# A Perceiver layer (attention, gated mixing, top-2 mixture of experts): router chain moved up by one batch, and a new order of work behind the loop

## The reference, cut to what matters

```
x = x + xattn(layernorm(x), ctx)          # 16 heads of 8, softmax over 257 keys
u = layernorm(x)                          # per batch of 32 rows:
xf = [u[0], u[1:] @ WB.T]; xb = [u[1:] @ WBf.T, u[-1]]
gamma = sigmoid(xf @ w1.T + xb @ w2.T + b)
x = x + gamma * (xf + xb) + (1 - gamma) * u
h = layernorm(x); logits = h @ gate        # 8 experts
w, e = top_k(logits, 2); w = softmax(w)
x = x + sum_k w_k * (silu(h @ w0[e_k]) * (h @ w1[e_k])) @ wo[e_k]
```

## Time and profile before

| what | us |
|---|---|
| median of 3 runs (lowest, highest) | 249.22 (248.66, 250.11) |
| the profiled execution, its own time | 247.98 |
| its span on the core | 246.2 |
| PE busy in the span | 211.2 (86%) |
| DVE, ACT, POOL busy | 145.7, 140.3, 131.0 |
| mean granted PE clock | 0.944 |

### The profile page before, as it was taken

How to read it: one execution, slowest core, us unless ns; L and a number is a source line. 1 busy time by engine, 2 the same in 40 slices (tenths; PEclk the granted TensorE clock), 3 DMA queues, 4 the chain that set the end, 5 groups by cost and what they waited for, 6 DMA issues and landing times.

```text
span 246.2 us, 6768 instructions
## 1 busy us (share of the span) xinstructions
PE 211.2 (86%) x2071; PEld 179.7 (73%) x2071; DVE 145.7 (59%) x521; ACT 140.3 (57%) x465; POOL 131.0 (53%) x334
## 2 busy tenths in 40 slices
PE   7789998999999999999994985539809999999970
PEld 7567777878777787778773684539809899999970
DVE  2788778788797887987968473234502123222602
ACT  2478878979888788887895642022402343444310
POOL 2874576854687686776864954062441233334303
PEclk9999999999999999999998699576977999999999
DMA  7799450500504600000002154304434877777053
GB/s 200 284 374 326 162 170 3 170 3 7 169 24 150 196 23 4 13 11 3 22 5 89 50 175 109 108 23 134 103 130 141 270 222 225 215 229 232 34 171 89
DMA packets 17763, 31.19 MB, mean 127 GB/s; under 512 B 2350, under 2 KB 9649, under 8 KB 17728
## 3 DMA queue, kind: packets, MB, share of 16 engines
q1 hardware_dynamic: 16112, 28.10, 36.5%
q0 software_dynamic: 1184, 2.12, 2.5%
q10 hardware_dynamic: 432, 0.54, 0.7%
HBM read 22.07 MB, written 9.01 MB: 126 GB/s over the span
## 4 chain that ended last, share of the span: by engine, by line
PE 53%; POOL 11%; DMA 11%; DVE 9%; issue 8%; ACT 4%; SPq 1%; POOLq 1%; ACTq 0%; DVEq 0%
PE bank L1119 13%; PE bank L1129 7%; PE bank L927 6%; PE bank L917 6%; PE bank L957 5%; PE bank L884 5%; PE bank L886 4%; DMA table<-rows_tok,slot_at 4%; DMA slot_sb<-table 3%; ACT p_sb L721 2%; DVE neg_max L1248 2%; POOL table L601 2%; DMA pt_sb<-planes 2%; POOL tile_rstd L556 2%; DMA vec_sb<-vectors 2%
## 5 line engine op out<-in xcount | busy, mean ns | idle before, releaser
L721 ACT ACTIVATE p_sb<-bank,neg_max 128x257 f32<-128x257 f32 x128 | 59.0, 472 | 21.6 <-DVE neg_max L1248 21.5
L1248 DVE TENSOR_REDUCE neg_max<-bank 128x1 f32<-128x257 f32 x128 | 48.6, 424 | 11.1 <-PE bank L996 5.2
L1119 PE MATMUL bank<-slot_ft,w_now 128*128 128x128 f32 x368 | 50.9, 287 | 0.6 <-issue 0.6
L1119 PEld LDWEIGHTS bank<-slot_ft,w_now 128*128 128x128 f32 x368 | 48.0, 204 | 1.6 <-issue 1.2
L667 POOL DMA_INDIRECT planes<-y_sb,y_row x21 | 20.8, 992 | 37.3 <-ACT y_sb L814 35.9
L1510 DVE TENSOR_TENSOR hid_ft<-silu_sb,bank 128x512 f32<-128x512 f32 x23 | 15.8, 687 | 37.0 <-PE bank L1119 36.1
L730 ACT ACTIVATE pt_sb<-bank 128x512 f32<-128x512 f32 x64 | 35.1, 612 | 1.2 <-PE bank L927 1.2
L927 PE MATMUL bank<-ident,p_sb 128*128 128x128 f32 x256 | 34.1, 277 | 0.0
L814 ACT ACTIVATE y_sb<-bank,zero_rows,slot_meta 128x128 f32<-128x128 f32 x23 | 10.5, 457 | 34.5 <-PE bank L1129 34.5
L927 PEld LDWEIGHTS bank<-ident,p_sb 128*128 128x128 f32 x256 | 29.7, 144 | 0.3 <-issue 0.3
L917 PE MATMUL bank<-kv_sb,qbd_sb 32*128 32x257 f32 x256 | 24.6, 425 | 3.5 <-ACT p_sb L721 1.4
(11 more groups left out here) (179 smaller groups left out, 333.9 us busy)
## 6 DMA issues: line engine op xcount, KB each, us to landing
w_now<-w SPq DMA_DIRECT2D x23, 512.0 KB, 4.0
table<-empty_rows SPq DMA_DIRECT2D x3, 1300.0 KB, 10.0
ctx_sb<-ctx_keys SPq DMA_DIRECT2D x7, 512.0 KB, 3.9
wo_sb<-wo SPq DMA_DIRECT2D x8, 256.0 KB, 4.3
slot_sb<-table SPq DMA_DIRECT2D x23, 65.0 KB, 2.8
planes<-zero_rows SPq DMA_DIRECT2D x2, 512.0 KB, 6.7
pt_sb<-planes SPq DMA_DIRECT2D x4, 256.0 KB, 4.8
table<-empty_rows SPq DMA_DIRECT2D x1, 975.0 KB, 10.1
```

The costliest lines, as they stand in the source:

```text
L721: act.activation(p_sb[b % 2][:, g, :], s_bank[g][:, 0:SKV], ACT.Exp, bias=neg_max[b % 2][:, g:g + 1], accum_out=sum_last[:, 0, b, g:g + 1] ...
L1119: last = pe.matmul(bank[2 * m + s % 2][:, tile(c)], w01_now[s % W_BUFS][:, m, tile(c)], slot_ft[s % 2][:], start=True, stop=True)
L1248: dve.tensor_reduce(neg_max[b % 2][:, g:g + 1], s_bank[g][:, 0:SKV], AX.X, ALU.max, negate=True).then_inc(max_ready, 1)
```

## The change

It has these parts (core of the diff below):

1. The six chain constants are one less, so that each chain step comes one batch earlier; `scale_tile`, `spread_scales`, `spread` and the taking of the spread scales also come one batch earlier. On POOL `spread_scales` moves to r = 0, ahead of `residual`; `count_experts` and `edges` are at r = 0 behind both; `tile_root(0)` is at r = 3, ahead of `queries`; `store_rows` is at r = 2.
2. The router works on the transposed unnormalised tile (`x2_tok`) and a centred gate matrix (`gate_c`, one product at b = 7); the softmax weight takes the inverse deviation as a scale. `turn_rows` waits for `x2_ready`, not for `rows_normed`.
3. `plan` is split in three parts; of `plan(0)` part 0 stands at the end of b = 29 and part 1 at the end of b = 30.
4. Behind the loop: another order on every engine, `keep_meta` and `number_output` are gone (row numbers and weights are read from the loaded rows, which have 131 columns instead of 130), the last `spread` writes to bank 1, four slot tiles (`LATE_TURNS`, one each) are transposed at the end of an iteration.
5. SP: 5 weight buffers and 8 row buffers; in each stage up to three weight loads are issued ahead of the row loads, in stage 0 too.
6. The planes are interleaved by token, read back with two DMAs of 512 KB; DVE adds the first pair, POOL the second.

```diff
-W_BUFS = 3
+W_BUFS = 5
-        WO_AT, TURN_AT, MIX_AT, ROW_TURN_AT, LOGITS_AT, RANKS_AT = 7, 8, 9, 11, 12, 13
+        WO_AT, TURN_AT, MIX_AT, ROW_TURN_AT, LOGITS_AT, RANKS_AT = 6, 7, 8, 10, 11, 12
@@ SP, in each stage
-                load_weights(first)
+                for s in range(first, heavy):          # heavy = min(end, first + 3)
+                    load_weights(s)
                 for i in range(stored, last_tile + 1):
                     sp.wait_ge(rows_stored[i], 16 * TOPK)
@@ SP, end
+            pairs = planes.rearrange("(p t c) d -> p t c d", p=128, c=TOPK)
             for n in range(2):
-                for c in range(TOPK):
-                    sp.dma_start(planes_sb[c][:, half_tiles(n), :], ...)
+                sp.dma_start(pairs_sb[n], pairs[:, half_tiles(n), :, :]).then_inc(pair_in[n], 16)
@@ POOL, loop over b
                 if r == 0 and b >= BPT:
+                    spread_scales(b // BPT - 1)
                     residual(b // BPT - 1)
...
                 if at(b, WO_AT + 1) is not None:
                     tile_root(0, at(b, WO_AT + 1))
                 if at(b, LOGITS_AT + 1) is not None:
                     count_experts(at(b, LOGITS_AT + 1))
                 if at(b, TURN_AT + 1) is not None:
                     edges(at(b, TURN_AT + 1))
-                if r == 1 and b > BPT:
-                    spread_scales(b // BPT - 1)
                 if at(b, MIX_AT + 1) is not None:
                     mix_residual(at(b, MIX_AT + 1))
                     tile_root(1, at(b, MIX_AT + 1))
                 if r == 3 and b // BPT + 1 < NT:
                     queries(b // BPT + 1)
@@ POOL, behind the loop
             add_heads(B - 2)
             add_heads(B - 1)
+            tile_root(0, NT - 2)
             count_experts(NT - 3)
             mix_residual(NT - 2)
+            edges(NT - 2)
+            keep_slots(NT - 3)
+            store_rows(NT - 3, 0)
             tile_root(0, NT - 1)
+            store_rows(NT - 3, 1)
+            mix_residual(NT - 1)
+            edges(NT - 1)
             tile_root(1, NT - 2)
@@ PE
             def turn_rows(i, dst):
-                pe.wait_ge(rows_normed, i + 1)
-                pe.transpose(dst[:, C_TURN], rows_tok[:, i, 0, 0:D], ident[:])...
+                pe.wait_ge(x2_ready, i + 1)
+                pe.transpose(dst[:, C_TURN], x2_tok[:, i, :], ident[:])...
             load_expert(0)
+            pe.wait_ge(pt0_ready, B)
             turn_slots(0)
-            pe.wait_ge(o_masked_ready, B)
-            spread(NT - 1)
+            weigh_values(B - 1)
+            spread(NT - 1, bank[1])
@@ DVE, loop over b
-                if b % BPT == 1 and b > BPT:
+                if b % BPT == 0 and b >= BPT:
                     scale_tile(b // BPT - 1)
-                if b == B - 2:
-                    plan(0)
...
                 if b >= 2:
                     take_output(b - 2)
+                if b == B - 3:
+                    plan(0, 0)
+                elif b == B - 2:
+                    plan(0, 1)
@@ DVE, behind the loop
-                if s + 1 < SLOT_TILES:
-                    keep_meta(s + 1)
-                before_hidden(s)
                 dve.wait_ge(silu_ready, s + 1)
                 dve.wait_ge(up_half_done, s + 1)
```

More of the change, by code:

```diff
@@ L380, in _ @@
                 first, end = first_slot_tile[k], first_slot_tile[k + 1]
-                ahead = min(end - first, W_BUFS if k == 0 else SLOT_BUFS - W_BUFS)
-                load_weights(first)
+                heavy = min(end, first + 3)
+                ready = min(end, first + 6)
+                for s in range(first, heavy):
+                    load_weights(s)
                 for i in range(stored, last_tile + 1):
@@ L615, in _ @@
                 if r == 0 and b >= BPT:
+                    spread_scales(b // BPT - 1)
                     residual(b // BPT - 1)
+                if b == B - 2:
+                    residual(NT - 1)
+                if b == B - 1:
+                    keep_last(b)
+                    add_heads(b - 2)
+                    spread_scales(NT - 1)
+                    continue
                 if at(b, WO_AT + 1) is not None:
@@ L630, in _ @@
                 if at(b, RANKS_AT + 2) is not None:
-                    store_rows(at(b, RANKS_AT + 2))
+                    keep_slots(at(b, RANKS_AT + 2))
+                    for c in range(TOPK):
+                        store_rows(at(b, RANKS_AT + 2), c)
                 if b >= 2:
@@ L786, in _ @@
                     turned(b - 1)
-                if at(b, WO_AT + 1) is not None:
+                if b + 1 < B and at(b, WO_AT + 1) is not None:
                     normalise(at(b, WO_AT + 1))
@@ L1161, in _ @@
                 between_halves(s)
-                if s + 1 < SLOT_TILES:
+                if s + 1 < SLOT_TILES and s + 1 not in LATE_TURNS:
                     turn_slots(s + 1)
                 half_hidden(s, 1)
+                behind_halves(s)
                 if s >= 1:
                     project(s - 1)
-                behind_halves(s)
-                if s > STORED:
-                    spread_late(s - 1)
+                behind_project(s)
+                if s + 1 in LATE_TURNS:
+                    turn_slots(s + 1)
             project(SLOT_TILES - 1)
-            spread_late(SLOT_TILES - 1)
+            for s in range(STORED, SLOT_TILES):
+                spread_late(s)
         @block.vector
@@ L1372, in take_slots, with plan @@
                 dve.tensor_reduce(slot_of[:, i, :], slot_part[:], AX.X, ALU.add).then_inc(slot_ready, 1)
-            def plan(k):
+            def plan(k, part):
                 tiles = STAGES[k][1]
@@ L1403, in _ @@
             for b in range(B):
-                finished = b // BPT - 1 if b % BPT == 3 and BPT <= b < B else None
+                finished = b // BPT - 1 if b % BPT == 2 and BPT <= b < B else None
                 maxima(b, finished)
```

365 lines of the change are left out of this document (184 added, 181 removed).

## The result

| what | before | after |
|---|---|---|
| median (lowest, highest) | 249.45 (248.66, 250.11) | 280.82 (278.22, 282.5) |
| span of the profiled execution | 246.2 | 280.8 |
| PE busy in it | 211.2 | 227.9 |
| mean granted PE clock | 0.944 | 0.899 |

The ratio is 1.1251, interval 1.1185 to 1.1318: slower, as forecast, but by 31 us instead of 9, and outside the range of 246 to 267. Every kernel here has faster and slower executions; ratios and intervals compare only the faster ones, so they can differ from the ratio of two medians.

What follows compares the result with a forecast made beforehand. PE was taken to bound the loop and last stage, the token chain the stretch between. Span: 246.2 + 27.9 - 0.3 - 13.7 - 3.4 (PE work already done) - 1.2 = 255.5 us, a median of about 258; range 246 to 267.

Steps and rivals of the forecast that it cites:

- Part 1: Loop: PE newly waits for POOL in two places of each cycle, costing 27.9 us more in all.
- the first place: Loop, r = 3: `scores` waits for `queries` behind `tile_root(0)`; new wait 2.1 us, six times, sum 11.9 us.
- the second: Loop, r = 0: `ranks` waits for `count_experts` behind `spread_scales` and `residual`; 2.9 us five times, sum 16.0 with b = 8.
- The 1.5 us of b = 8: Loop, b = 8: `edges` but no count; the wait exceeding the 1.1 us of `keys_values`, taken as 1.5 us.
- rival C: Loop: PE's clock falls once a cycle behind the new waits, 5 x 2 us more, 268 us; chance 0.15.
- part 3: Chain from slot tile 0's first product (H) to slot tile 7's rows: H+29.2 instead of H+42.9, gain 13.7 us.
- A: Loop: the first place's wait is absorbed as DVE runs ahead, 246 us; both places absorbed, 230; chance 0.15.
- B: Behind the loop: the chain shrinks to PE's own work, 250 us, slot tile 7 at H+25 or less; chance 0.12.
- D: Slot tile 0 starts no earlier because weight loads take 6 us: 3 us more, 261; chance 0.58 together with the forecast.
- Part 2: Loop end to slot tile 0: -1.7 for `weigh_values`, -1.6 for moved PE work, +3 for weight loads; sum -0.3 us.
- Part 4: End: two 512 KB reads replace four of 256 KB and DVE takes one of POOL's additions; gain 1.2 us.

Runs made afterwards that it cites:

- spread_behind: Changed kernel with POOL doing `count_experts` and `edges` ahead of `spread_scales` and `residual` at r = 0; 254.6 us, ratio 1.0116 to the kernel before.
- queries_first: Changed kernel with POOL computing `queries` ahead of `tile_root(0)` at r = 3; 260.67 us against 248.71 for the kernel before.
- before_spread_ahead: Kernel before with POOL's `spread_scales` moved ahead of `count_experts` and `edges` at r = 1; 271.56 us against 249.13 for the kernel before.
- warm_waits: Changed kernel, POOL untouched, nine unread identity products ahead of each waiting `scores` (b = 11 on) and each `ranks`; 267.82 us, ratio 1.0754 to the kernel before.
- before_spread_filled: before_spread_ahead with nine identity products ahead of each `ranks`; 261.13 us, ratio 1.0479 to the kernel before.
- both_orders: Changed kernel with both POOL edits, those of queries_first and spread_behind; 241.7 us, ratio 0.9654 to the kernel before.
- one_weight_stage0: both_orders with SP issuing one weight load, not three, ahead of the slot rows in the first stage only; 237.43 us, ratio 0.9443 to the kernel before.
- warm_slots_half: both_orders with 15, 8, 4 and 11 identity products ahead of the waits for four slot tiles' rows; 240.13 us, ratio 0.9644 to the kernel before.
- warm_slots: both_orders with 30, 16, 8 and 22 identity products ahead of the waits for rows of slot tiles 0, 3, 5, 7; 245.11 us, ratio 0.9845 to the kernel before.
- one_weight_warm: warm_slots with SP also issuing one weight load, not three, ahead of the slot rows in every stage; 246.14 us, ratio 0.9872 to the kernel before.
- both_orders_5: both_orders measured again, unchanged; 245.08 us, ratio 0.967 to the kernel before.

## Why the prediction was wrong in size

**Part 1, the waits: right.** Place, releaser, number and length were as laid out: 16.0 us six times and 10.5 us five times, against 12.7 in all (11.9 of it new) and 14.5; each place alone 12.1 and 14.7. In the kernel after the first place is longer (up to 3.3) and the second shorter (up to 2.6) than worked out, probably because DVE's steps slip with the slowed PE; the sum is 26.5 against 27.2. The 1.5 us of b = 8 came as 0.3.

**The step that failed: the price of PE's clock, left out of the sum.** The sum took the waits at their bare length. The clock stood beside it as rival C, with a chance of 0.15 and a price of 5 x 2 = 10 us, one drop a cycle. Measured: 19.8 us, by PE's busy time in the loop over the 114.7 of before, useful work alone. The fourth column counts the waits behind which the granted clock of the next few microseconds is below 1.00:

| kernel | new waits | us of waits | clock lost behind | busy time more |
|---|---|---|---|---|
| spread_behind | 6 | 12.1 | 3 | 6.6 |
| queries_first | 5 | 14.7 | 4 | 8.2 |
| before_spread_ahead | 5 | 13.2 | 4 | 7.8 |
| after | 11 | 26.5 | 9 | 19.8 |
| warm_waits | 10 of 11 filled | | | 1.7 |
| before_spread_filled | 5, filled | | | 1.8 |

The clock is lost behind a wait or it is not, and within these lengths the length of the wait does not decide it. In spread_behind the six waits are alike, 2.00 to 2.07 us, and take turns; each of these windows (columns as in the earlier trace rows) runs from the end of such a wait to the next `scores`, and the last two waits, not shown, give 0.69 and 1.00 again:

```profile
41.96:47.47 5.51, 5.51 (x43) 4.75 (x43) 2.62 (x8) 3.27 (x11) 2.67 (x14) 0.69 0.02 3
61.58:65.30 3.72, 3.72 (x41) 2.97 (x41) 2.40 (x9) 2.41 (x10) 0.73 (x5) 1.00 0.00 0
79.43:84.97 5.54, 5.54 (x42) 4.56 (x42) 3.09 (x11) 3.20 (x11) 1.44 (x10) 0.69 0.01 3
98.71:102.43 3.72, 3.72 (x42) 2.97 (x42) 2.40 (x9) 2.41 (x10) 0.72 (x5) 1.00 0.00 0
```

The same 41 to 43 products take 3.7 us or 5.5. In queries_first five waits of 2.94 us each lose it four times; the second and the third:

```profile
84.39:91.03 6.64, 6.64 (x49) 5.66 (x49) 2.94 (x10) 3.13 (x12) 1.82 (x9) 0.57 0.48 161
105.06:112.33 7.27, 7.23 (x86) 5.80 (x87) 5.40 (x18) 5.41 (x21) 3.76 (x16) 1.00 0.01 2
```

In after the waits of 1.60 and 2.63 us keep it and one of 1.78 loses it. What decides is open, and it changes between executions: the lowest runs of spread_behind (250.7), queries_first (256.0) and after (278.2) lie 13, 18 and 40 us above the lowest of the kernel without the waits (238.0, both_orders), so about 1, 3 and 14 us above the length of their waits. The table has one profiled execution of each, for spread_behind the slowest of its five.

A lost clock costs 2.0 to 2.2 us on average (last column over the fourth), so C's price of one drop was right; its number was wrong, nine and not five, and so was leaving it outside the sum. I had a row of either side, low after 3.40 us and not after 0.79, and the new waits lay between. Both things that C and the forecast say (clock below 1.0 in the loop, 27.9 us of waits) could be true at once, and were: C is an addition to the forecast, not another way in place of it, and 258 + 20 = 278 would have been the sum. In spans it is 255.5 + 19.8 = 275.3 against 280.8, and of the 5.5 us still missing 5.3 are those of part 3. The rule of the Trainium skill ("TensorE: Matmul & The Clock Gate", Part 1), that the low clock is the default and only activity lifts it, agrees with these runs: behind 20 of 27 idle spells of 1.6 to 3.3 us the clock was below 1.00, and identity products in them held it at 0.99 to 1.00.

**Rivals A and B fell:** no wait was absorbed, cycles were 22.7 to 25.5 us and not under 18; slot tile 7 was transposed at H+34.5 and not at H+25. What D names, the weight loads, was there with 3.9 us, close to the 3 in the sum.

**Part 2: near in the sum, by luck.** It gave +0.2 against -0.3, but 1.65 us of it are counted in the loop: of the 3.40 us in front of `weigh_values`, 1.65 are left (-1.75, taken as -1.7), and they now lie ahead of `scores(31)`. With them it is +1.9. PE's busy time behind `scores(31)` is 1.7 us less (8.61 to 6.89, taken as 1.6). New are 2.62 us for ACT, which nobody forecast, and 3.23 us for the rows of slot tile 0. The end of the loop in the profile after, SP and PE:

```profile
175.07 0.67 PE L977 MATMUL bank<-pt_sb,kv_sb 128*32 128x128 f32 x16 [1.65 <-DVE keys_part L1335]
...
179.14 2.56 SPq L372 DMA_DIRECT2D w_now<-w  x3
...
181.28 1.06 PE L947 MATMUL bank<-ident,p_sb 128*128 128x128 f32 x8 [2.62 <-ACT pt_sb L747]
...
182.61 2.51 SPq L380 DMA_DIRECT2D slot_sb<-table  x3
...
186.29 0.30 PE L1132 MATMUL bank<-ident,slot_sb 128*128 128x128 f32 x1 [3.23 <-DMA slot_sb<-table]
```

3.7 us from the issue of the first rows to their use. The chain of waits goes through the rows, not through ACT: PE would have stood for them anyway. one_weight_stage0 shows that the loads cost 3.9 us there, where I took 3, with bounds of 0 and 6.

**Part 3: right in kind, 5.3 us short.** The gain was 8.4 us, below the lower bound of 9. The forecast itself was added up 0.4 us too low: H+23, 4.8 and 1.8 make H+29.6. POOL, the new order and SP kept the schedule: slot tile 7's rows were asked for at H+28.1 (forecast H+27.4), and no DVE wait for slot rows was left. Then two things came. The landing was not 1.8 us where it decides: the chain of waits of both_orders has

```profile
170.11 4.62 DMA table<-rows_tok,slot_at
...
175.45 4.03 DMA slot_sb<-table
```

4.0 us, behind three weight loads issued since 170.47 (its H is 146.85, the transpose 179.53: H+32.7). And in the profile after PE was not ready: ACT stood still for 3.97 us at H+21 with a releaser that the profile can't name ("another core or an unknown queue" in the chain), PE waited 1.69 us for its copy and then ran at a clock of 0.50 until H+32:

```profile
209.74 3.97 another core or an unknown queue
...
214.41 2.08 PE bank L1145 x8
```

It is not in both_orders; one_weight_stage0 and warm_slots_half have one of 3.9 and 3.8 us before the same `y_sb`, that of slot tile 3. How much of the 5.3 us is its doing, and its cause, stay open. The last stretch gave 4.0 us of the predicted 4.6.

**Part 4: right.** The reads are issued at 270.66 and the last addition ends at 278.10, 7.4 us; before it was 8.6. The 1.2 us are those of the forecast, and the first read was in use 4.1 us after its issue (270.66 to 274.71), where I took 4.0. The Trainium skill ("DMA: Bandwidth & Descriptors", section "Anatomy of one DMA"), named in the prediction for such a read, gives its formula for DMAs that GpSimd issues; these are issued by SP, so they don't test it, and no term hangs on it.

```profile
270.66 0.81 SPq L401 DMA_DIRECT2D pt_sb<-planes  x2
...
277.41 0.69 DVE L1546 TENSOR_TENSOR norm_tok<-bank,pt_sb 128x512 f32<-128x512 f32 x1 [1.22 <-POOL pt_sb L699]
```

No run undid this part by itself.

## What to carry to other kernels

Where PE is the bound, price a new wait as its length plus the slow products behind it, in the sum and not beside it: here waits of 1.6 to 3.3 us lost the clock in 20 of 27 cases of the profiled executions, at 2.0 to 2.2 us each, so a wait between a row that kept the clock and a row that lost it is to be taken as losing it. When a chain is moved by a step, order each engine's new neighbours by who waits for them: a wide operation that nobody needs soon belongs behind the 0.2 us operation for which the busiest engine stands. And a load that is issued early "because it can" sits ahead of the small one that is urgent: one ahead, the rest behind, was worth 3.9 us here, 1.7 of them because SP is free to ask sooner.

## What the runs showed of the hardware

- Useless work can pay: nine identity products (2.27 us) in each long wait made the kernel 13 us faster in warm_waits, and 10.4 us by the medians (5.9 by the lowest runs) in before_spread_filled. Past the end of the waits they cost something, though less than their length: 3.4 us for 7.7 us too much in warm_slots, 8.9 for 15.5 in one_weight_warm.
- The same wait can lose the clock or keep it: of six waits of 2.00 to 2.07 us in one execution three lost it, of five of 2.94 us four.
- The two places seem to cost more together than apart: 19.8 us of slow work in after, 6.6 + 8.2 = 14.8 in the kernels with one each. It goes with the count of lost clocks, nine against three and four, in one profile of each kernel; why there are more is open.
- Kernels with such waits tend to scatter: from lowest to highest run queries_first 11.4 us, spread_behind 8.8 and before_spread_ahead 8.1, against 3.2 for warm_waits and before_spread_filled. It is no rule: after has 4.3, and both_orders_5, with a clock of 1.00 in the loop, 7.7.
- ACT can stand still for 3.8 to 4.0 us without a releaser in the profile, in three of the fourteen profiles, each time at `y_sb` of slot tile 3; DVE stands 1.5 to 1.6 us under the same mark in the same profiles. In the DMA view of after from 205 to 216 us no queue that carries instructions moves anything, so a fetch of code is not seen there.
